# Full-array score matmuls over zero-padded operands, new orders, and one subtraction moved from VectorE to GpSimd

## The chip, the cores and the metric

One core of a Trainium2 chip runs the whole program. The metric is the device time of one execution in microseconds, the median of the runs shown.

## The reference

A pre-norm transformer layer on x of 16 sequences by 256 tokens by 256 features, in float32:

```python
x = x + attention(layernorm(x))      # 16 heads of 16; key j is masked where j - i > 16
x = x + ffn(layernorm(x))
# attention: q, k, v = z @ w.T ; softmax(q k^T / 4 + mask) v, then @ wo.T
# ffn: silu(z @ gate_w.T) * (z @ up_w.T) @ down_w.T, inner width 1024
# gate_w, up_w, down_w: cubic splines through 2033 control points each
```

## The kernel before, in words

**Turns.** One turn is one sequence of 256 tokens, so there are 16 turns (t). A turn is cut into steps: `la`, `lb` (layer norm), `zt` (transpose), `qk` (two halves of 8 heads), `v`, `ld` (DMAs that lay out the queries and keys), `s1` (scores for the row maximum, eight steps of two heads), `mt` (the maxima turned), `sc` (transposed scores and exponential, eight steps), `av` (weighted sums, four steps of four heads), `ot` (division and turning), `on` (splitting in high and low parts), `wo`, `ma`, `mb`, `z2`, `mo` (moments for the spline weights), `ga`, `up`, `ic`, `dn`, `y` (the feed-forward part and the result). Some nine tenths of the columns of TensorE are float32r matmuls in three products (high by high, high by low, low by high), so every operand is held as a rounded high part (ScalarE copies it) and a low remainder (a subtraction).

**Order.** Tables `START`, `OWN` and `TURN` give each step a number; the steps of all turns are sorted by it (`all_steps`), and each engine issues its share of every step in that order. Nothing reorders an engine's queue: a step whose input is late holds all behind it on that engine. Several turns are in work at once. In the middle turns a `s1` step of one turn and a `sc` step of the turn before follow each other on TensorE; such a pair is called a couple below.

**Scores.** A float32 product of 16 features in three terms is one contraction over 64 rows: every fourth partition holds the high part, the low part, or the high part again. `ld` (L661 to L671) fills `QM` and `KS`, each [128, slot of the turn, pair, 256], with 6 DMAs per half and 12 per turn; the slot is t % 2, so two turns have their own space. Two heads of a pair lie in partitions 0 to 63 and 64 to 127. A `s1` step (L1026 to L1035) and a `sc` step (L1042 to L1050) are four matmuls, two for each head, that use half the rows of the array each; the two heads write different banks of PSUM. `mt` (L1036, L904 to L909, L672 to L677) turns 16 columns twice, copies 16 by 256, and two DMAs put the negated maxima in row 63 of each half of `QM`, which `sc` multiplies with a row of ones in `KS`. PSUM gives these steps two places (`pairs`), each seeded with the mask by ScalarE before a `s1` step.

**Around them.** SP issues all DMAs: 12 for `ld`, 2 for `mt`, the loads `x` and `xr` and the store `y`: 17 in a turn, and 24 more (`pm`, L656) at the start. `on` is a copy on ScalarE and a subtraction on VectorE (L847). GpSimd does `affine_select` on the exponentials in two instructions after every second `sc` step (L732, L735), a power in `la` and `ma`, and the low half of `ic` (L740).

Of the kernel before, what the change touches and what calls it, by code (L numbers as in the profile page):

```python
# [7 lines left out]
F32 = mybir.dt.float32  # L8
# [7 lines left out]
H, DH = 16, 16  # L16
# [19 lines left out]
HP = NP // 2  # L36
DMA = 16
# [4 lines left out]
NQ = NW // 128  # L42
POWERS = 4
# [141 lines left out]
PERIOD = 29.3  # L185


def steps(table):

    return [(what, n + by * i, at + gap * i) for what, n, count, by, at, gap in table for i in range(count)]  # L190


START = [("fill", 0, 1, 1, -150.464, 0), ("hot", 0, 1, 1, -108.040, 0), ("in", 0, 1, 1, -104.078, 0),
             ("fill", 1, 1, 1, -103.866, 0), ("hot", 1, 1, 1, -101.965, 0), ("tap", 0, 1, 1, -86.665, 0),
             ("split", 0, 1, 1, -83.421, 0), ("in", 4, 1, 1, -81.659, 0), ("hot", 2, 1, 1, -72.688, 0),
# [3 lines left out]
             ("fill", 3, 1, 1, -49.605, 0), ("hot", 3, 1, 1, -45.788, 0), ("fill", 4, 1, 1, -45.146, 0),  # L199
# [3 lines left out]
             ("wj", 4, 1, 1, -33.201, 0), ("hot", 4, 1, 1, -29.039, 0), ("hot", 5, 1, 1, -26.819, 0),  # L203
# [939 lines left out]
```

## Time and profile before

| | |
|---|---|
| median of 3 runs | 530.36 us (530.16 to 531.9) |
| span of the profiled execution, first to last instruction | 529.3 us |
| its own device time beside the span | not given apart; the median is 1.1 us above the span |
| busy: PE, PEld, DVE, ACT, POOL | 507.1, 435.1, 425.4, 364.7, 211.9 us |
| mean granted TensorE clock | 0.987 |
| DMA: bytes, mean rate | 44.51 MB, 84 GB/s |

Busy is the union of an engine's instructions. Matmuls overlap in the pipeline, so their cost is read from start to start, not from their durations. Two matmuls that start within some nanoseconds of each other run side by side. SPq is SP's issuing of DMAs, which counts as no engine's busy time.

### The profile page before, as it was taken

The numbers are of one execution on the slowest core, as the hardware profiler recorded it, in microseconds if no ns is written. First come the engines' busy times: TensorE is split into PE (matmuls) and PEld (weight loads), VectorE is DVE, ScalarE is ACT, GpSimd is POOL, SyncE is SP. The second block draws the span as 40 slices with busy tenths as digits, with TensorE's granted clock in tenths as the row PEclk, the third lists the DMA queues.
The fourth block names the chain that finished last, engine by engine and source line by source line (L and its number), as shares of the span: only waits on it lengthen the run. The fifth ranks groups of instructions, "written<-read, shape, count | busy, mean of one in ns | idle before, by whom it ended". The sixth has DMA issues, their size and how long they took to land.

```text
span 529.3 us, 12741 instructions
## 1 busy us (share of the span) xinstructions
PE 507.1 (96%) x4840; PEld 435.1 (82%) x4840; DVE 425.4 (80%) x944; ACT 364.7 (69%) x536; POOL 211.9 (40%) x255
## 2 busy tenths in 40 slices
PE   7997979999999999999999999999999999999896
PEld 4665757898888898888888898988898888888785
DVE  4585679898898988898998998888988877777853
ACT  3366788676767778686877778686868777775522
POOL 4853345424343342424333352424343333435413
PEclk9898999999999999999999999999999999999999
DMA  8552332214032313131222123133212121300100
GB/s 257 202 179 69 125 101 73 70 50 145 28 113 73 99 62 122 63 120 63 89 84 75 58 81 102 62 100 102 82 60 81 46 78 37 106 2 22 41 21 20
DMA packets 45500, 44.51 MB, mean 84 GB/s; under 512 B 4736, under 2 KB 44544, under 8 KB 45440
## 3 DMA queue, kind: packets, MB, share of 16 engines
q1 hardware_dynamic: 45440, 43.70, 25.0%
q8 instruction: 39, 0.64, 0.5%
q14 instruction: 21, 0.17, 0.1%
HBM read 13.01 MB, written 4.19 MB: 33 GB/s over the span
## 4 chain that ended last, share of the span: by engine, by line
PE 70%; DVE 9%; SPq 9%; DMA 4%; issue 3%; ACT 3%; POOL 1%; POOLq 0%; DVEq 0%; ACTq 0%
PE ring L978 9%; PE ring L979 7%; PE ring L980 7%; PE ring L1056 7%; PE pair L1033 6%; PE pair L1048 6%; PE ring L1087 5%; SPq L670 4%; PE ring L1088 4%; PE ring L1089 4%; SPq L656 3%; DVE M L902 3%; PE ring L971 3%; PE ring L962 2%; PE ring L1076 2%
## 5 line engine op out<-in xcount | busy, mean ns | idle before, releaser
L806 ACT ACTIVATE P<-pair 128x800 f32<-128x800 f32 x128 | 106.4, 837 | 46.6 <-PE pair L1048 37.3
L902 DVE TENSOR_REDUCE M<-pair 128x2 f32<-128x288 f32 (+1 forms) x256 | 133.3, 565 | 2.9 <-PE pair L1033 2.7
L740 POOL TENSOR_TENSOR IN<-GU,IN 128x512 fp32r<-128x512 f32 x64 | 82.6, 1293 | 129.9 <-ACT IN L745 129.4
L745 ACT ACTIVATE pair<-SEED 128x800 f32<-128x800 bf16 x128 | 107.6, 842 | 14.1 <-DVE M L902 10.3
L732 POOL TENSOR_SCALAR_AFFINE_SELECT P<-P 128x448 f32<-128x448 f32 x64 | 37.3, 583 | 120.8 <-ACT P L806 120.8
L978 PE MATMUL ring<-WD,IN 128*128 128x256 f32 x256 | 76.4, 299 | 1.4 <-POOL IN L740 1.1
L1087 PE MATMUL ring<-Y,WGUh 128*128 128x256 f32 x256 | 76.2, 298 | 0.7 <-DVE Y L847 0.4
L1088 PE MATMUL ring<-Y,WGUh 128*128 128x256 f32 x256 | 72.0, 281 | 0.0
L1089 PE MATMUL ring<-Y,WGUl 128*128 128x256 f32 x256 | 71.8, 281 | 0.0
L979 PE MATMUL ring<-WD,IN 128*128 128x256 f32 x256 | 71.6, 280 | 0.0
L980 PE MATMUL ring<-WD,IN 128*128 128x256 f32 x256 | 71.6, 280 | 0.0
L745 ACT ACTIVATE IN<-GU 128x512 fp32r<-128x512 f32 x64 | 39.9, 627 | 29.5 <-DVE GU L948 28.9
L1048 PE MATMUL pair<-QM,KS 64*128 64x256 f32 (+1 forms) x512 | 53.5, 293 | 5.9 <-DMA QM<-MT 5.1
L1033 PE MATMUL pair<-KS,QM 63*128 63x256 f32 (+1 forms) x512 | 54.1, 294 | 3.0 <-ACT pair L745 1.5
L1087 PEld LDWEIGHTS ring<-Y,WGUh 128*128 128x128 f32 x256 | 48.2, 188 | 6.1 <-issue 3.0
L978 PEld LDWEIGHTS ring<-WD,IN 128*128 128x128 f32 x256 | 48.1, 188 | 5.7 <-issue 2.4
L1056 PE MATMUL ring<-P,V 128*32 128x256 f32 (+1 forms) x1024 | 52.2, 337 | 0.0
L1048 PEld LDWEIGHTS pair<-QM,KS 64*128 64x128 f32 x512 | 38.4, 188 | 16.6 <-issue 8.8
L1033 PEld LDWEIGHTS pair<-KS,QM 63*128 63x128 f32 x512 | 38.0, 186 | 15.9 <-ACT pair L745 6.2
L943 DVE SCALAR_TENSOR_TENSOR GU<-GU,ring 128x512 f32<-128x512 f32 x64 | 43.5, 681 | 8.7 <-ACT GU L831 7.7
L1089 PEld LDWEIGHTS ring<-Y,WGUl 128*128 128x128 f32 x256 | 48.2, 188 | 0.0
L1088 PEld LDWEIGHTS ring<-Y,WGUh 128*128 128x128 f32 x256 | 48.2, 188 | 0.0
(94 smaller groups left out, 1171.0 us busy)
## 6 DMA issues: line engine op xcount, KB each, us to landing
QM<-QK SPq DMA_DIRECT2D x96, 128.0 KB, 2.1
KS<-QK SPq DMA_DIRECT2D x96, 128.0 KB, 2.1
X<-x SPq DMA_DIRECT2D x32, 256.0 KB, 2.9
out<-X SPq DMA_DIRECT2D x16, 256.0 KB, 2.2
OVERD<-over_down SPq DMA_DIRECT2D x2, 512.0 KB, 7.6
PO<-W SPq DMA_DIRECT2D x16, 48.0 KB, 2.2
P<-wqk SPq DMA_DIRECT2D x2, 256.0 KB, 5.9
QM<-MT SPq DMA_DIRECT2D x32, 8.0 KB
```

Of the source, the lines that this page charges most:

```text
L745: copy = lambda dst, src: nc.scalar.activation(dst, src, ACT.Copy)
L806: nc.scalar.activation(P[:, g % 2, 2 * (n % 2):2 * (n % 2) + 2, :], pair(what, t, n)[:, :, 0:SW], ACT.Exp, scale=SCALE).then_inc(exp_done, 1)
L902: i = nc.vector.tensor_reduce(out=M[:, t % 2, it, :].rearrange("p (a k) -> p a k", a=2)[:, :, n], in_=pr[:, :, cols], axis=AX.X, op=ALU.ma ...
L978: mm(b, act(k, 0), w[:, k, 0:D], start=first and k == 0, stop=False, skip_group_check=True)
L979: mm(b, act(k, 0), w[:, k, D:2 * D], start=False, stop=False, skip_group_check=True)
L980: i = mm(b, act(k, 1), w[:, k, 0:D], start=False, stop=False, skip_group_check=True)
L1033: i = mm(pr[:, a, c:c + w], QM[r, t % 2, n, it * 128:(it + 1) * 128], KS[r, t % 2, n, 0:w], start=False, stop=it == 0, skip_group_check=True)
L1048: i = mm(pr[:, a, c:c + w], KS[r, t % 2, n, jt * 128:(jt + 1) * 128], QM[r, t % 2, n, S - w:S], start=jt == 0, stop=jt == 1, skip_group_ch ...
L1056: i = mm(bk[32 * hl:32 * hl + 32, S - w:S], V[:, t % 2, jt, n * 4 + hl, :, :].rearrange("p a c -> p (a c)"), P[:, n % 2, hl, c:c + w], sta ...
L1087: mm(o, wh, y[:, 0, g, :], start=j == 0, stop=False, skip_group_check=True)
L1088: mm(o, wh, y[:, 1, g, :], start=False, stop=False, skip_group_check=True)
L1089: i = mm(o, wl, y[:, 0, g, :], start=False, stop=False, skip_group_check=True)
```

## The change

- `s1` and `sc` are two matmuls each. The moving operand is a new tile, `KZ` and `QZ`, [128, 2, 4, 2, 256]: for head a of a pair only the 64 partitions of that head are filled, and the others hold zeros. One matmul with all 128 rows gives both heads side by side, 512 columns in one bank, and 288 in the next.
- Each of `QM`, `KS`, `QZ`, `KZ` has one copy in place of a slot per turn parity. `QK`, the source, has two. `ld` is 9 DMAs per half (three of 128 KB, six of 64 KB) and loads `QM` and `KZ`; it waits for `s1` of the turn before. A new step `lk` is 9 DMAs (three of 256 KB, six of 128 KB) for `KS` and `QZ`; it waits for all `sc` steps of the turn before. `mt` is one transpose of 128 columns, a copy of 32 by 128, and two DMAs into `QZ`.
- The subtraction of `on` goes from VectorE to GpSimd. `affine_select` is issued after every `sc` step over half the elements.
- `Z`, `OT` and `Y` have one copy instead of two. The small tiles of the layer norm have four.
- `START`, `OWN` and `TURN` have new numbers throughout.

```diff
-PERIOD = 29.3
+PERIOD = 29.4252
-TURN = [("x", 0, 1, 1, -56.556, 0), ("la", 0, 1, 1, -41.879, 0), ("lb", 0, 1, 1, -38.839, 0),
+TURN = [("x", 0, -90.4333), ("la", 0, -72.8908), ("lb", 0, -52.8920), ("zt", 0, -46.4935), ("qk", 0, -23.4598),
...
-        QM = sb("QM", [128, 2, NP, S], F32R)
-        KS = sb("KS", [128, 2, NP, S], F32R)
-        QK = sb("QK", [128, 2, 2, 2 * S], F32R)
+        QM, KS = (sb(n, [128, HP, 2, S], F32R) for n in ("QM", "KS"))
+        QZ, KZ = (sb(n, [128, 2, HP, 2, S], F32R) for n in ("QZ", "KZ"))
+        QK = [sb(f"QK{i}", [128, 2, 2, 2, S], F32R) for i in range(2)]
...
+        def heads_of(pr):
+            return ((pr[:, 0, :].rearrange("p (a c) -> p a c", a=2), S),
+                    (pr[:, 1, 0:2 * W1].rearrange("p (a c) -> p a c", a=2), W1))
...
                 elif what == "ld":
-                    sp.wait_ge(cleared, 4 if t else 2)
-                    if t >= 2:
-                        sp.wait_ge(sc_made, nth("sc", t - 2, n * HP + HP - 1))
+                    sp.wait_ge(cleared, 2)
+                    if t:
+                        sp.wait_ge(s1_made, nth("s1", t - 1, n * HP + HP - 1))
                     sp.wait_ge(qk_low, nth("qk", t, n))
...
+                    for k, part in enumerate(Q_PARTS):
+                        sp.dma_start(QM[k:128:4, :, n, :].bitcast(F32), QK[t % 2][:, part, 0, n, :].bitcast(F32)).then_inc(
+                            kz_loaded[n], DMA)
+                    for k, part in enumerate(K_PARTS):
+                        for a in range(2):
+                            r = slice(STACK * a, STACK * (a + 1))
+                            sp.dma_start(KZ[STACK * a + k:STACK * (a + 1):4, a, :, n, :].bitcast(F32),
+                                         QK[t % 2][r, part, 1, n, :].bitcast(F32)).then_inc(kz_loaded[n], DMA)
+                elif what == "lk":
+                    sp.wait_ge(cleared, 4)
+                    if t:
+                        sp.wait_ge(sc_made, nth("sc", t - 1, NP - 1))
+                    sp.wait_ge(qk_low, nth("qk", t, 1))
+                    for k, part in enumerate(K_PARTS):
+                        sp.dma_start(KS[k:128:4].rearrange("p j h c -> p j (h c)").bitcast(F32),
+                                     QK[t % 2][:, part, 1].rearrange("p h c -> p (h c)").bitcast(F32)).then_inc(ks_loaded, DMA)
+                    for k, part in enumerate(Q_PARTS):
+                        for a in range(2):
...
                 elif what == "mt":
                     sp.wait_ge(mt_done, nth("mt", t, 0))
+                    if t:
+                        sp.wait_ge(sc_made, nth("sc", t - 1, NP - 1))
...
-                elif what == "sc" and n % 2:
+                elif what == "sc":
...
+                elif what == "on":
+                    pool.wait_ge(on_high, nth("on", t, 0))
+                    low(OTT[:, 1, :, :], OT[:, 0:KB, :], OTT[:, 0, :, :]).then_inc(on_low, 1)
...
                 elif what == "s1":
-                    for it, c, w in ((1, W0, S), (0, 0, W0)):
-                        for a in range(2):
-                            r = slice(STACK * a, STACK * a + STACK - 1)
-                            i = mm(pr[:, a, c:c + w], QM[r, t % 2, n, it * 128:(it + 1) * 128], KS[r, t % 2, n, 0:w],
-                                   start=False, stop=it == 0, skip_group_check=True)
+                    h, j = divmod(n, HP)
+                    if j == 0:
+                        pe.wait_ge(kz_loaded[h], N_LOAD * (t + 1))
+                    for it, (o, w) in zip((1, 0), heads_of(pair(what, t, n))):
+                        i = mm(o, QM[:, j, h, it * 128:(it + 1) * 128], KZ[:, :, j, h, 0:w], start=False, stop=True, skip_group_check=True)
...
                 elif what == "sc":
+                    h, j = divmod(n, HP)
                     if n == 0:
-                        pe.wait_ge(m_loaded[t % 2], N_M * (t // 2 + 1))
+                        pe.wait_ge(ks_loaded, N_LOAD * (t + 1))
+                        pe.wait_ge(m_loaded, N_M * (t + 1))
+                    for jt, (o, w) in enumerate(heads_of(pair(what, t, n))):
+                        i = mm(o, KS[:, j, h, jt * 128:(jt + 1) * 128], QZ[:, :, j, h, S - w:S], start=True, stop=True)
```

How the order moves is shown at two places of a middle turn. First TensorE, where the turned maxima of the turn stand. `KS,QM` is a `s1` step and `QM,KS` a `sc` step of the kernel before; `P,V` is `av`, `ID,M` the transposes of the maxima, `WD,IN` a `dn` step. `Y,WGUh` and `Y,WGUl` belong to `ga` and `up`. Before, a couple stands between an `up` and a `dn` step:

```order
L1089 MATMUL ring<-Y,WGUl 128x256
L1033 MATMUL pair<-KS,QM 128x256 x2
L1033 MATMUL pair<-KS,QM 128x144 x2
L1048 MATMUL pair<-QM,KS 128x256 x2
L1048 MATMUL pair<-QM,KS 128x144 x2
L978 MATMUL ring<-WD,IN 128x256
```

Of the change (`KZ,QM` is `s1`), the maxima stand next to `av`:

```order
L1050 MATMUL ring<-Y,WGUl 128x256
L998 MATMUL pair<-KZ,QM 128x512
L998 MATMUL pair<-KZ,QM 128x288
L1002 MATMUL ring<-ID,M 128x128
L1017 MATMUL ring<-P,V 32x256 x4
L1017 MATMUL ring<-P,V 32x144 x4
L1017 MATMUL ring<-P,V 32x256 x4
L1017 MATMUL ring<-P,V 32x144 x4
L998 MATMUL pair<-KZ,QM 128x512
L998 MATMUL pair<-KZ,QM 128x288
L945 MATMUL ring<-WV,ZT 128x256
```

A score step went from four rows to two, and the couples are mostly dissolved: of 256 steps, 132 runs of neighbouring score steps became 227. `av` has 42 runs before and 43 now; 24 of them directly followed a score step before, with no change of the array's shape in between.

Second SP, one middle turn. Before:

```order
L684 DMA out<-X 128x2x256
L681 DMA X<-x 128x2x256
L670 DMA QM<-QK 32x4x256 x3
L670 DMA KS<-QK 32x4x256 x3
L660 DMA X<-x 128x2x256
L676 DMA QM<-MT 1x8x256 x2
L670 DMA QM<-QK 32x4x256 x3
L670 DMA KS<-QK 32x4x256 x3
```

Of the change:

```order
L639 DMA X<-x 128x2x256
L619 DMA KS<-QK 32x4x512 x3
L624 DMA QZ<-QK 16x4x512 x6
L599 DMA X<-x 128x2x256
L642 DMA out<-X 128x2x256
L634 DMA QZ<-MT 1x16x128 x2
L606 DMA QM<-QK 32x4x256 x3
L611 DMA KZ<-QK 16x4x256 x6
L606 DMA QM<-QK 32x4x256 x3
L611 DMA KZ<-QK 16x4x256 x6
```

SP issues 32 DMAs in a turn instead of 17, and between the last `sc` step of one turn and the first of the next now stand nine of `lk`, one or two of x and out, and the two of the maxima.

## Rows read from the trace of the kernel before

**Rows 1.** The page, part 1: busy time, share of the span, instructions.
```profile
...
PE 507.1 (96%) x4840; PEld 435.1 (82%) x4840; DVE 425.4 (80%) x944; ACT 364.7 (69%) x536; POOL 211.9 (40%) x255
```

**Rows 2.** Windows: busy PE, PEld, DVE, ACT, POOL (instructions), clock, DMA share, GB/s.
```profile
...
0.00:20.00 20.00, 17.25 (x79) 11.29 (x80) 10.70 (x26) 6.08 (x9) 11.65 (x14) 0.83 0.79 264
236.00:265.00 29.00, 29.00 (x292) 25.51 (x291) 25.52 (x59) 21.66 (x33) 11.18 (x14) 1.00 0.23 74
500.00:529.00 29.00, 22.27 (x176) 20.85 (x174) 13.82 (x26) 8.53 (x15) 8.71 (x8) 1.00 0.06 19
```

**Rows 3.** Timeline of PE around one couple of score steps: start, duration, instruction, count.
```profile
...
246.32 0.28 PE L1088 MATMUL ring<-Y,WGUh 128*128 128x256 f32 x1
246.44 0.28 PE L1089 MATMUL ring<-Y,WGUl 128*128 128x256 f32 x1
246.65 0.45 PE L1033 MATMUL pair<-KS,QM 63*128 63x256 f32 x4
246.94 0.39 PE L1048 MATMUL pair<-QM,KS 64*128 64x256 f32 x4
247.26 0.39 PE L978 MATMUL ring<-WD,IN 128*128 128x256 f32 x1
247.48 0.28 PE L979 MATMUL ring<-WD,IN 128*128 128x256 f32 x1
```

**Rows 4.** Timeline of PE, a run of full-array bf16 matmuls of 256 columns.
```profile
...
19.96 1.49 PE L992 MATMUL ring<-HEAT 128*128 128x256 bf16 x12
```

**Rows 5.** Timeline of PE: a double weighted sum, the maxima's transposes; the next turn's.
```profile
...
240.76 0.28 PE L1089 MATMUL ring<-Y,WGUl 128*128 128x256 f32 x1
240.97 1.56 PE L1056 MATMUL ring<-P,V 128*32 128x256 f32 x32
242.46 0.39 PE L1039 MATMUL ring<-ID,M 128*16 128x128 f32 x2
242.83 0.39 PE L1087 MATMUL ring<-Y,WGUh 128*128 128x256 f32 x1
243.06 0.28 PE L1088 MATMUL ring<-Y,WGUh 128*128 128x256 f32 x1
...
271.95 0.39 PE L1039 MATMUL ring<-ID,M 128*16 128x128 f32 x2
```

**Rows 6.** Groups by line and shape: busy us, mean ns of one, idle before.
```profile
...
L847 DVE TENSOR_TENSOR OTT<-OT,OTT 128x512 fp32r<-128x512 f32 x16 | 11.8, 737 | 1.8 <-ACT OTT L745 1.3
...
L909 DVE CAST MT<-ring 16x256 fp32r<-16x256 f32 x16 | 6.1, 383 | 1.1 <-PE ring L1039 1.1
...
L745 ACT ACTIVATE OTT<-OT 128x512 fp32r<-128x512 f32 x16 | 10.1, 631 | 6.5 <-DVE OT L925 6.5
...
L740 POOL TENSOR_TENSOR IN<-GU,IN 128x512 fp32r<-128x512 f32 x64 | 82.6, 1293 | 129.9 <-ACT IN L745 129.4
```

**Rows 7.** Timeline of SP, the DMA issues of one stretch.
```profile
...
258.74 0.39 SPq L684 DMA_DIRECT2D out<-X  x1
...
263.62 2.70 SPq L670 DMA_DIRECT2D KS<-QK  x3
266.37 0.59 SPq L660 DMA_DIRECT2D X<-x  x1
273.29 1.43 SPq L676 DMA_DIRECT2D QM<-MT  x2
274.83 1.88 SPq L670 DMA_DIRECT2D QM<-QK  x3
```

**Rows 8.** The chain that ended last, at the maxima's load in turn 2.
```profile
...
97.23 1.95 DMA QM<-MT
...
99.32 0.69 PE pair L1048 x8
```

**Rows 9.** Windows: the stretch with most DMA traffic beside the loads.
```profile
...
289.20:293.00 3.80, 3.80 (x34) 3.55 (x35) 3.30 (x7) 3.71 (x6) 0.79 (x2) 1.00 0.83 273
```

**Rows 10.** Waits of PE from 120 to 440 us: total, times, longest.
```profile
...
PE pair L1048 <- DMA QM<-MT: 0.2, 1, 0.2
```

More of the change, by code:

```diff
@@ L36 @@
 HP = NP // 2
+EDGE = 2 * S
+PS = 2 * SW
 DMA = 16
@@ L398, in all_steps @@
 def all_steps():
-    out = [(at, what, 0, n) for what, n, at in steps_of_start()]
-    out += [(t * PERIOD + at, what, t, n) for t in range(TURNS) for what, n, at in steps_of_turn(t)]
+    out = [(at, what, 0, n) for at, what, n in steps_of_start()]
+    out += [(t * PERIOD + at, what, t, n) for t in range(TURNS) for at, what, n in steps_of_turn(t)]
     return [i[1:] for i in sorted(out, key=lambda i: i[0])]
@@ L530, in build @@
         GU = sb("GU", [128, 2, 2 * S])
-        Y = [sb(f"Y{i}", [128, 2, 3, S], F32R) for i in range(2)]
+        Y = sb("Y", [128, 2, 3, S], F32R)
+        YT = sb("YT", [128, 2, KB, S], F32R)
         ring = [ctx.enter_context(nc.psum_tensor(f"ring{i}", [128, 512], F32)) for i in range(4)]
@@ L542, in build @@
         mo_made, mo_high, mo_low = map(sem, ("mo_made", "mo_high", "mo_low"))
-        qk_loaded = [[sem(f"qk_loaded{s}{h}") for h in range(2)] for s in range(2)]
-        m_loaded = [sem(f"m_loaded{s}") for s in range(2)]
+        kz_loaded = [sem(f"kz_loaded{h}") for h in range(2)]
+        ks_loaded, m_loaded = map(sem, ("ks_loaded", "m_loaded"))
         xr_loaded, y_stored = ([sem(f"{n}{i}") for i in range(N_X1)] for n in ("xr_loaded", "y_stored"))
@@ L781, in _ @@
                     act.wait_ge(qk_made, nth("qk", t, n))
-                    if t:
-                        act.wait_ge(qk_loaded[(t - 1) % 2][n], N_QK * ((t - 1) // 2 + 1))
-                    copy(QK[:, n, 0, :], bank(what, t, n)[:]).then_inc(qk_high, 1)
+                    if t >= 2:
+                        act.wait_ge(kz_loaded[n], N_LOAD * (t - 1))
+                        act.wait_ge(ks_loaded, N_LOAD * (t - 1))
+                    copy(QK[t % 2][:, 0, :, n, :], halves(bank(what, t, n)[:])).then_inc(qk_high, 1)
                 elif what == "v":
@@ L797, in _ @@
                         act.wait_ge(*emptied(BEFORE["s1", t, n]))
[L798 removed]
+                    copy(scores(pair("s1", t, n)), SEED[:]).then_inc(seeded, 1)
                 elif what == "sc":
@@ L811, in _ @@
                         act.wait_ge(wo_made, nth("wo", t - 1, 0))
-                    copy(OTT[:, 0, :, :], OT[t % 2][:, 0:KB, :]).then_inc(on_high, 1)
+                    copy(OTT[:, 0, :, :], OT[:, 0:KB, :]).then_inc(on_high, 1)
                 elif what == "z2":
                     act.wait_ge(z2_made, nth("z2", t, 0))
+                    if t == 0:
+                        act.wait_ge(permuted, 24 * DMA)
                     if t:
@@ L822, in _ @@
                         act.wait_ge(ws_low, GATE_UP)
-                    if t >= 2 and n == 0:
-                        act.wait_ge(up_made, nth("up", t - 2, 3))
+                    if t and n == 0:
+                        act.wait_ge(up_made, nth("up", t - 1, 3))
                     g = slice(2, 3) if n else slice(0, 2)
-                    copy(Y[t % 2][:, 0, g, :], moments(bank(what, t, n), n)).then_inc(mo_high, 1)
+                    copy(Y[:, 0, g, :], moments(bank(what, t, n), n)).then_inc(mo_high, 1)
                 elif what == "ga":
@@ L894, in _ @@
                     dve.wait_ge(qk_high, nth("qk", t, n))
-                    low(QK[:, n, 1, :], bank(what, t, n)[:], QK[:, n, 0, :]).then_inc(qk_low, 1)
+                    low(QK[t % 2][:, 1, :, n, :], halves(bank(what, t, n)[:]), QK[t % 2][:, 0, :, n, :]).then_inc(qk_low, 1)
                 elif what == "s1":
                     dve.wait_ge(s1_made, nth("s1", t, n))
-                    pr = pair("s1", t, n)
+                    if n == 0 and t == 0:
+                        dve.wait_ge(m_cleared, 1)
                     if n == 0 and t >= 2:
                         dve.wait_ge(mt_made, nth("mt", t - 2, 0))
-                    for it, cols in ((0, slice(0, W0)), (1, slice(W0, W0 + S))):
-                        i = nc.vector.tensor_reduce(out=M[:, t % 2, it, :].rearrange("p (a k) -> p a k", a=2)[:, :, n],
-                                                    in_=pr[:, :, cols], axis=AX.X, op=ALU.max, negate=True)
+                    for it, (o, w) in zip((1, 0), heads_of(pair("s1", t, n))):
+                        k = n % HP * 4 + n // HP * 2 + it
+                        i = nc.vector.tensor_reduce(out=M[:, t % 2, 0:2 * H].rearrange("p (a k) -> p a k", a=2)[:, :, k],
+                                                    in_=o, axis=AX.X, op=ALU.max, negate=True)
                     i.then_inc(max_done, 1)
@@ L1132 @@
         "ident": np.eye(128, dtype=np.float32),
-        "seed": np.concatenate([np.zeros((128, AHEAD)), upper, np.zeros((128, W0)), upper[:, :J1]], axis=1).astype(ml_dtypes.bfloat16),
+        "seed": np.concatenate([np.zeros((128, W0)), upper[:, :J1]] * 2 + [np.zeros((128, AHEAD)), upper] * 2, axis=1).astype(ml_dtypes.bfloat16),
     }
```

143 lines of the change are left out of this document (66 added, 77 removed), and 297 rows, old and new, of tables (OWN, START, TURN).

## The prediction

> **What bounds the kernel now.** I read the page's busy times first: TensorE 96%, VectorE 80%, ScalarE 69%, GpSimd 40% [rows 1]. The windows say where. In a middle turn TensorE is busy all of the 29 us, at a granted clock of 1.00, and VectorE 25.5 of it; in the first 20 us it has 17.25 us at clock 0.83, and in the last 29 us 22.27 [rows 2]. From 120 to 440 us the only wait that TensorE has on a DMA is 0.2 us, for the maxima [rows 10]. So in the middle the work that TensorE has per turn is the time per turn: the transposes of the maxima of neighbouring turns start at 242.46 and 271.95, 29.49 us apart [rows 5]. What shortens TensorE's queue shortens the kernel, unless something else becomes late; what changes on VectorE or GpSimd alone does not.
>
> **The score steps.** Full-array matmuls of 256 columns start 0.12 us apart (246.32, 246.44). After the last, the couple should start at 246.56. It starts at 246.65, its second step at 246.94, the next full matmul at 247.26, and the one behind that only at 247.48 instead of 0.12 later [rows 3]. The couple thus holds the engine from 246.56 to 247.48 - 0.12 = 247.36: 0.80 us. The step itself is some 0.23 us, and 0.35 us of the 0.80 is the passage into half-array work (0.09) and out of it (0.26, of which 0.10 shows only on the second full matmul). 128 couples make 102.4 us. 24 runs go straight on to a weighted sum, which is also narrow, and save the 0.10 once: 100 us.
>
> After, a step is 512 and 288 columns on the whole array, without a passage. At the pace of the full float32r matmuls (0.12 for 256) that is 0.37 us; at 2.4 GHz and one column a cycle 800 columns need 0.33 us. The bf16 matmuls of 256 columns are nearer to the latter: 12 of them span 1.49 us, of which the last one's own pipeline is some 0.28, so they start 0.11 apart [rows 4]. The float32r ones lose 0.01 more on each, and a matmul twice as long pays that once for 512 columns. I take 0.35, so 256 steps make 89.6 us, with 84.5 to 94.7 as bounds. **Gain 10.4 us.**
>
> The rule that speaks against this stands in the Trainium skill, "TensorEngine Tiling (Array Packing)", section "Theoretical Speedup": with a contraction of at most 64 rows, row tiling gives up to twice the speed, so giving it up should cost. The rows show why it need not: the two halves do run side by side (a step of 800 columns in all in 0.23 us), but the passages take back more than that. The same page, "Key Properties", says that changing the mode drains the engine; by that rule, the trace agrees, with the 0.35 us per couple.
>
> **Weighted sums and maxima.** `av` stays narrow. Two steps take from 240.97 to 242.46, and entering costs 0.21 - 0.12 = 0.09 [rows 5]. Before, 24 of its 42 runs came from a score step and paid no entry; now all 43 do: 25 x 0.09 = 2.2 us, and six more exits at 0.10: 0.6 us. **Loss 2.8 us.** Of the two transposes of the maxima one goes: 16 x 0.12 = 1.9 us, and where the narrow shape left late (242.46 to 242.83 for two, then 0.23) another 0.2 in some turns: **gain 2.4 us.** TensorE's queue is thus shorter by 10.4 - 2.8 + 2.4 = **10 us**, with bounds of 5 and 15 from the step's. In a middle turn this is 0.6 us.
>
> **VectorE, GpSimd, ScalarE.** VectorE loses 16 subtractions of 0.737 us and about 0.1 us per copy of the maxima [rows 6]: under the full TensorE this is worth nothing. GpSimd takes 1.293 us for such a subtraction of 128 by 512 [rows 6], so `wo` gets its input 0.56 us later. In a middle turn 6.8 us of other work stand on TensorE between the last weighted sum and `wo` (`v` and two `qk` of 12 matmuls each, four score steps, a `mo` and a `ga`), and the chain of transposes, division, copy and subtraction adds to 4 us, or 6.2 with two reductions between. Cover is left; without it 0.56 x 16 = 9 us would be lost. GpSimd has 11.2 of 29 us busy [rows 2] and goes to some 14: nothing. The single `Z`, `OT` and `Y` are asked for 7 us or more after they come free in the new table: nothing. ScalarE has the same 800 elements per seed and exponential.
>
> **SP and the single buffers.** This is the change's cost. An issue takes 0.62 us (three in 1.88), one of the maxima's 0.71, one of out 0.39, one of x 0.59 [rows 7]. 32 issues are 20 us of a turn of 29, so SP is not full. But `lk` may only start when the last `sc` step of the turn before has ended, and the maxima's DMAs are behind it. The chain from the end of the last `sc` to the first `sc` of the next turn: 0.35 to see the matmul's end; nine issues 5.6; x or out or both 0.4 to 1.0; the first maxima DMA's issue 0.74; the second's issue and landing 1.95, and 0.14 until TensorE starts [rows 8]. Together 9.2 to 9.8 us. In that time TensorE has, by the new order of the middle turns, two `up` steps, three `s1` steps, the maxima, two weighted sums, a fourth `s1`, `v`, two `qk`, a `mo` and a `ga`: 10 us. That covers it barely. It fails where the order has less: turn 2 (9.6 us of work, two loads of x), turn 13 (8.9), turn 15 (8.9), and turn 1, where six `pm` DMAs stand in between (13.2 against 11.5). I add 1.7 + 0.3 + 0.6 + 0.2 = 2.8 us. One issue in about 25 takes 0.4 to 1.7 us longer (2.70 for three at 263.62) [rows 7]; with 12 issues in each of 15 chains that is some 6 us, half of it covered: 2.7. **Loss 5.5 us**, lower bound 0 (all covered), upper bound in the rival below.
>
> **Start and end.** New orders there too. The fills before the first `ld` grow from two memsets to the size of three, while GpSimd waits for weights anyway. SP's queue until the maxima of turn 1 has some 80 issues instead of 64, but 12 of the 24 `pm` move behind them. By the same issue times the first `sc` of turn 2 comes at about 95 to 101 us, against 99.32 now [rows 8]. The last turn has 5 us more of TensorE work behind its maxima, but was a stretch with 7 us idle [rows 2]. I set both at 0, from -4 to +5.
>
> **Sum.** 529.3 - 10 + 5.5 = 524.8 us of span, and with the 1.1 us by which the median of the runs lies above the span, **525.9 us**, 0.8% under 530.36.
>
> **Rivals.**
> *The single buffers hold TensorE in every turn (slower).* For it: the loads of `lk` are 1.5 MB, with x and out 2 MB in 6.5 us, 310 GB/s, and the densest stretch now moved 273 GB/s at a DMA share of 0.83 [rows 9], so at most 329. If the queue runs at 273, the maxima land 1 us later or more; and if a `lk` issue costs 0.71 like those of the maxima, 0.8 us comes on top. 1.2 us over the cover in 15 turns is 18 us in place of 5.5: 538 us. It decides from 0.65 us per turn, where TensorE's 10 us are gone. Against: 64-partition transfers may be issued faster, and half the excess comes with HBM transfers that do not stand in every chain.
> *The packing was worth its passages.* If a full step costs twice the 0.23 us of the packed one, 256 x 0.46 = 118 us against 100: the queue grows by 18 instead of shrinking by 10, 554 us. Against: the columns of the full matmuls around it go at 0.12 for 256, which leaves no room for it. This is the tiling page's twofold speed taken at its word.
> *All of it comes through.* Steps at 0.33 us, waits covered, a start 3 us earlier: 529.3 - 15 + 1 - 3 + 1.1 = 513 us. For it: VectorE is relieved, and the order was laid out for these lengths.
> *No change beyond measurement.* Gains and waits cancel: 530.4 us. Likewise if the matmul's gain is at its lower bound of 5.
>
> **How the numbers follow.** A measurement of this kernel tells about 0.3% from no change: 528.8 to 532.0. Forecast 0.52, all through 0.13, no change 0.13, held by the single buffers 0.19, packing 0.03. Of the forecast's own spread (step 0.33 to 0.37, start and end) little lies above 528.8. So faster 0.65, same 0.13, slower 0.22. The range takes in the forecast's bounds and most of the first rival: 514 to 538 us.
>
> **What would show it.** Right: score steps of 0.34 to 0.36 us from start to start with full matmuls 0.12 us before and behind them; middle turns of 28.8 to 29.2 us; waits of TensorE on the load into `QZ`, some 5 us in all; the first `sc` of turn 2 near 98 us. The forecast is wrong if a wait on `QZ` stands in every middle turn, if middle turns stay at 29.5 with TensorE full (the step is dearer than 0.37), or if the first maxima of turn 2 are turned much after 95 us.

## The result, and the profile after

The changed kernel takes 538.78 us (median of 4 runs, 537.08 to 541.22), beside 530.38 for the kernel before on the same chip: a ratio of 1.015, 95% interval 1.0118 to 1.0183. It is 1.5% slower, where 525.9 was forecast, and lies 0.8 us above the range. The profiled execution took 537.08 us, its span is 535.4 against 529.3: 6.1 of the 8.4 us can be looked for in the traces. Of the other 2.3, 1.7 us are that the profiled execution was quicker than the median of its kernel. Of the kernels' executions shown here all are in the fast state; one more of `e5_packed`, of 1585 us, was in the slow one and is left out.

The busy line of the profile's page, to be read against [rows 1]:

```profile
...
PE 503.7 (94%) x4312; PEld 441.7 (83%) x4312; DVE 428.9 (80%) x929; ACT 356.2 (67%) x536; POOL 256.3 (48%) x399
```

TensorE has 3.4 us less of busy time in a span that is 6.1 us longer. So the idle time grew, and the windows tell where (columns as in [rows 2]):

```profile
...
0.00:20.00 20.00, 8.29 (x38) 5.50 (x38) 11.66 (x19) 4.00 (x5) 8.44 (x10) 0.78 0.53 179
236.00:265.00 29.00, 28.74 (x263) 26.34 (x262) 25.12 (x58) 21.20 (x33) 13.55 (x24) 1.00 0.43 143
...
0.00:192.36 192.36, 168.77 (x1275) 134.92 (x1276) 147.70 (x318) 122.76 (x183) 96.57 (x140) 0.95 0.46 150
```

In the first 20 us TensorE has 8.29 us of work done, before it was 17.25. The middle turn is nearly full, as before. The last row reaches to the maxima of turn 5: TensorE has 23.6 us without work in it. In the kernel before it has 12.2 up to the same place.

A place in the program that both kernels have is the transpose of the maxima (L1039 before, L1002 after). Its times cut the span into three:

| us | turn 5's maxima | turn 15's maxima | end | 0 to turn 5 | ten turns | rest |
|---|---|---|---|---|---|---|
| before | 184.1 | 473.7 | 529.3 | 184.1 | 289.6 | 55.6 |
| after | 192.4 | 480.2 | 535.4 | 192.4 | 287.8 | 55.2 |
| difference | | | | **+8.3** | **-1.8** | -0.4 |

**The loss is made before turn 5**, where the forecast has a zero. The first `sc` of turn 2 comes at 107.5 us, not at 95 to 101.

The marks cut the span by time and not by work, and the order is new. Counted in the traces, the changed kernel has less ahead of turn 5's maxima: two steps of `av`, 12 matmuls of `dn`, 12 of `ga` and `up`, 4 of `mo` and 24 of `qk`, against one `s1` step more. At the paces of a middle turn that is some 7 us of work (an estimate). It has some 2 us more between the two marks and 5 us more behind them. So 8.3 us is the least that the start lost, and the ten turns gained more than 1.8.

Four turns hold the same matmuls in both kernels but for the score steps and the maxima: from turn 6's maxima to turn 10's. The windows for the kernel before, for the changed one, and for the run `e6_issue_order` below, where TensorE never waits in them:

```profile
...
213.00:331.00 118.00, 118.00 (x1181) 104.09 (x1178) 105.08 (x239) 89.06 (x129) 45.48 (x58) 1.00 0.25 82
```

```profile
...
222.90:339.30 116.40, 114.99 (x1046) 105.74 (x1044) 101.44 (x231) 84.84 (x128) 54.34 (x92) 1.00 0.41 135
```

```profile
...
219.10:333.80 114.70, 114.70 (x1047) 105.63 (x1045) 101.52 (x231) 84.68 (x128) 54.37 (x92) 1.00 0.41 137
```

Without a wait a turn is 0.83 us shorter than before. With the waits of the changed kernel 0.4 us of it are left.

**The start, first part.** TensorE's waits in the whole run (total, times, longest):

```profile
...
PE ring L929 <- DVE X L856: 10.5, 1, 10.5
PE pair L1009 <- DMA QZ<-MT: 6.1, 8, 1.4
```

One wait of 10.5 us, on the normalised `X` (before 0.9). VectorE and GpSimd in that time (start, duration, instruction, count):

```profile
...
6.18 0.75 DVE L843 BATCH_NORM_STATS2 ST<-X 128x6 f32<-128x256 f32 x2 [4.71 <-DMA X<-x]
...
9.38 7.16 DVE L856 TENSOR_SCALAR X<-X,MV,RSTD 128x256 f32<-128x256 f32 x4 [0.81 <-POOL RSTD L659]
```

```profile
...
9.64 1.26 POOL L649 TENSOR_TENSOR WQKl<-P,WQKh 128x512 fp32r<-128x512 f32 x1 [0.30 <-ACT WQKh L708]
10.85 3.65 POOL L662 MEMSET KZ<- 128x4096 f32 x1
14.45 1.95 POOL L662 MEMSET QM<- 128x2048 f32 x1
```

```profile
...
L856 DVE TENSOR_SCALAR X<-X,MV,RSTD x4: 411/1660/3674, 9.4 to 14.6; 128x256 f32<-128x256 f32 x4
```

Four normalisations of 128 by 256 take 7.16 us. The shortest is 0.411 us, the other three are 1.352, 3.674 and 1.967 us, and beside them lie GpSimd's subtraction (1.26 us) and its two memsets (3.65 and 1.95 us). The pairs match in length and in time. The Trainium skill, "SBUF — State Buffer", section "Who interferes with whom", has the rule: a `tensor_scalar` on VectorE can run in a mode that uses the port pair shared with GpSimd, and whichever of the two is issued first holds it for the whole instruction. The trace agrees: the memset of 3.65 us begins at 10.85, the normalisation behind it at 10.98, and that ends 0.15 us after the memset. In the kernel before, both memsets (1.80 us each) were over by 4.50 us, ahead of VectorE's first normalisation at 6.07. In the new table they stand behind GpSimd's share of the layer norm. Also, `X` of turn 0 is now the third transfer and turn 1 is normalised first, so VectorE starts at 6.18 instead of 3.48 us.

TensorE had nothing to do from 6.2 to 16.7 us. Its granted clock fell to 1.2 GHz at 11.2 us and was back at 2.4 GHz at 25 us, so its first work ran at the lower one, with full matmuls of 256 columns 0.21 us apart and not 0.12. In the kernel before it was also down, from 11.0 to 17.8 us, and both kernels have short stretches of it later. Up to turn 5 TensorE was busy for 15.0 us at the lower clock, before for 13.7. Nearly half of such time is lost, so the clock itself explains some 0.7 us of the difference (an estimate).

**The start, second part.** SP's queue (issues: start, duration, count), and its waits from 20 to 105 us, after and then before:

```profile
...
65.53 3.14 SPq L611 DMA_DIRECT2D KZ<-QK  x5
68.78 2.14 SPq L619 DMA_DIRECT2D KS<-QK  x3
70.96 4.19 SPq L624 DMA_DIRECT2D QZ<-QK  x6
75.19 4.05 SPq L595 DMA_DIRECT2D PO<-W  x6
79.29 0.58 SPq L599 DMA_DIRECT2D X<-x  x1
79.97 1.18 SPq L634 DMA_DIRECT2D QZ<-MT  x2
81.19 7.58 SPq L595 DMA_DIRECT2D PO<-W  x12
```

```profile
...
SPq L599 <- PE ring L929: 3.7, 1, 3.7
SPq L617 <- PE pair L1009: 1.5, 1, 1.5
SPq L634 <- DVE MT L879: 0.6, 2, 0.3
```

```profile
...
SPq L665 <- PE pair L1048: 15.0, 3, 8.5
SPq L660 <- PE ring L962: 11.0, 1, 11.0
SPq L676 <- DVE MT L909: 2.9, 2, 2.7
SPq L665 <- DVE QK L847: 1.8, 2, 1.6
```

Before, SP waited for others for 30.7 of these 85 us, with 83 issues that took 52.3 us. After, it has 118 issues of 73.3 us in all and waits 5.8 us: from 25 us on it is nearly always behind. The 12 moves into `WP` (`PO<-W` in the rows) at 81.19, and six more at 75.19, stand between the loads for the scores.

**The middle.** A score step between full matmuls (as [rows 3]), and the chain from the loads of `KS` to the first `sc` of turn 7 (start, duration, piece):

```profile
...
235.52 0.28 PE L1050 MATMUL ring<-Y,WGUl 128*128 128x256 f32 x1
235.64 0.53 PE L1009 MATMUL pair<-QZ,KS 128*128 128x512 f32 x2
236.01 0.28 PE L1048 MATMUL ring<-Y,WGUh 128*128 128x256 f32 x1
236.13 0.28 PE L1049 MATMUL ring<-Y,WGUh 128*128 128x256 f32 x1
```

```profile
...
250.01 0.55 SPq L619
...
251.91 0.60 SPq L624
...
257.25 0.56 SPq L634
...
257.86 2.33 DMA QZ<-MT
...
260.32 0.47 PE pair L1009
```

The step holds the engine from 235.64 to 236.01, 0.37 us, and the matmul behind it starts 0.12 later as it should: there is no passage any more. In the chain, `KS` is issued from 250.01, 0.35 us after the `sc` that it waits for, and TensorE starts at 260.32: 10.7 us, the last 0.3 of them a wait; the longest such wait in the run is 1.4 us.

### The profile page after: what moved, and what is told of

It is laid out like the page before. It is cut to its first block, busy times and chain, and to the rows that moved or that the text cites. A ratio compares the mean times of both kernels' runs of the same rounds, so it can differ in the third digit from the quotient of the medians.

```text
span 535.4 us, 12091 instructions
## 1 busy us (share of the span) xinstructions
PE 503.7 (94%) x4312; PEld 441.7 (83%) x4312; DVE 428.9 (80%) x929; ACT 356.2 (67%) x536; POOL 256.3 (48%) x399
## 4 chain that ended last, share of the span: by engine, by line
PE 67%; SPq 16%; DVE 6%; DMA 5%; issue 3%; ACT 2%; POOL 1%; DVEq 0%
PE pair L1009 8%; PE ring L945 7%; PE ring L946 7%; PE ring L947 7%; PE pair L998 6%; PE ring L1017 6%; SPq L624 5%; PE ring L1048 5%; PE ring L1050 5%; PE ring L1049 5%; DMA QZ<-MT 4%; SPq L611 3%; SPq L619 3%; PE ring L929 2%; PE ring L1037 2%
## 5 line engine op out<-in xcount | busy, mean ns | idle before, releaser
L872 DVE TENSOR_REDUCE M<-pair 128x2 f32<-128x512 f32 (+1 forms) x256 | 132.4, 564 | 9.8 <-PE pair L998 8.7
L692 POOL TENSOR_SCALAR_AFFINE_SELECT P<-P 128x224 f32<-128x224 f32 x128 | 49.2, 385 | 125.9 <-ACT P L770 125.8
L703 POOL TENSOR_TENSOR IN<-GU,IN 128x512 fp32r<-128x512 f32 x64 | 81.9, 1294 | 55.4 <-ACT IN L708 55.2
L998 PE MATMUL pair<-KZ,QM 128*128 128x512 f32 (+1 forms) x256 | 72.6, 368 | 5.8 <-ACT pair L708 3.7
L1009 PE MATMUL pair<-QZ,KS 128*128 128x512 f32 (+1 forms) x256 | 70.5, 361 | 7.0 <-DMA QZ<-MT 6.1
L1048 PE MATMUL ring<-Y,WGUh 128*128 128x256 f32 x256 | 72.4, 283 | 0.0
L945 PE MATMUL ring<-WD,IN 128*128 128x256 f32 x256 | 72.1, 281 | 0.1
L946 PE MATMUL ring<-WD,IN 128*128 128x256 f32 x256 | 72.0, 281 | 0.0
L947 PE MATMUL ring<-WD,IN 128*128 128x256 f32 x256 | 71.8, 280 | 0.0
L1049 PE MATMUL ring<-Y,WGUh 128*128 128x256 f32 x256 | 71.6, 280 | 0.0
L998 PEld LDWEIGHTS pair<-KZ,QM 128*128 128x128 f32 x256 | 39.1, 189 | 18.8 <-ACT pair L708 10.0
L695 POOL TENSOR_SCALAR_AFFINE_SELECT P<-P 128x256 f32<-128x256 f32 x128 | 53.8, 420 | 0.0
L1009 PEld LDWEIGHTS pair<-QZ,KS 128*128 128x128 f32 x256 | 39.6, 191 | 13.3 <-issue 7.9
L945 PEld LDWEIGHTS ring<-WD,IN 128*128 128x128 f32 x256 | 48.1, 188 | 1.8 <-issue 0.2
L947 PEld LDWEIGHTS ring<-WD,IN 128*128 128x128 f32 x256 | 48.2, 188 | 0.0
```

The lines of the kernel that those rows point to most:

```text
L872: i = nc.vector.tensor_reduce(out=M[:, t % 2, 0:2 * H].rearrange("p (a k) -> p a k", a=2)[:, :, k], in_=o, axis=AX.X, op=ALU.max, negate=True)
L945: mm(b, act(k, 0), w[:, k, 0:D], start=first and k == 0, stop=False, skip_group_check=True)
L946: mm(b, act(k, 0), w[:, k, D:2 * D], start=False, stop=False, skip_group_check=True)
L947: i = mm(b, act(k, 1), w[:, k, 0:D], start=False, stop=False, skip_group_check=True)
L998: i = mm(o, QM[:, j, h, it * 128:(it + 1) * 128], KZ[:, :, j, h, 0:w], start=False, stop=True, skip_group_check=True)
L1009: i = mm(o, KS[:, j, h, jt * 128:(jt + 1) * 128], QZ[:, :, j, h, S - w:S], start=True, stop=True)
```

## The experiments

The theories after the result. *Start*: the port pair and the order of the first transfers, then SP's full queue. *Rival 1*: the single buffers hold TensorE all along. *Rival 2*: the packing was worth more than its passages. *Rival 3*: GpSimd's subtraction is not free. All ratios are to the kernel before on the same chip, with 95% intervals; its median there was 530.4 to 531.9 us. Beside the times, the table gives the turns' marks as above, all runs but `e4` in the changed kernel's order on TensorE. The marks are those of one profiled execution each, and executions of one kernel differ (those of e2 by 7 us), so what a run is worth is read from its ratio, and a mark says where it was gained.

| run | time, us | ratio | turn 5 | turn 15 | span |
|---|---|---|---|---|---|
| after | 538.78 | 1.015 [1.0118, 1.0183] | 192.4 | 480.2 | 535.4 |
| e1_fills_first | 534.29 | 1.0025 [0.9998, 1.0052] | 189.4 | 479.1 | 534.3 |
| e2_start_order | 532.08 | 0.9994 [0.9965, 1.0023] | 188.1 | 474.6 | 530.0 |
| e3_on_vector | 537.56 | 1.0098 [1.0062, 1.0134] | 190.9 | 478.9 | 534.3 |
| e4_order_before | 601.55 | 1.1278 | 231.4 | 540.0 | 601.2 |
| e5_packed | 562.23 | 1.0558 [1.0511, 1.0606] | 195.6 | 502.0 | 557.0 |
| e6_issue_order | 531.03 | 0.9988 [0.9967, 1.001] | 189.1 | 473.1 | 528.6 |
| e7_ks_scalar | 536.06 | 1.0095 [1.0065, 1.0125] | 193.4 | 480.6 | 536.0 |
| e8_pm_scalar | 541.91 | 1.0189 [1.0155, 1.0223] | 199.5 | 486.4 | 542.0 |
| e9_pm_once | 527.98 | 0.993 [0.9903, 0.9957] | 185.1 | 469.0 | 524.2 |
| e10_merged_loads | 524.97 | 0.9872 [0.9843, 0.99] | 185.7 | 469.4 | 524.3 |
| e11_best | 530.6 | 0.9978 [0.9957, 0.9999] | 187.3 | 471.3 | 526.6 |

### The memsets first

```diff
-START = [... ("fill", 0, -141.4603), ... ("fill", 1, -135.8028),
+START = [... ("fill", 0, -500.0), ... ("fill", 1, -499.0),
```

> The changed kernel with its first two fills (KZ, QM) put at the head of GpSimd's queue, ahead of the powers of the first two layer norms. Theory A (the start: the fills run beside VectorE's first normalisations, and each of these lasts as long as the fill beside it, 1.4, 3.7 and 2.0 us instead of 0.41): the four normalisations take 1.6 us instead of 7.2, the first transposes start at about 11 us instead of 16.7, and the time falls by 4 to 6 us, to 533 to 535 us. Theory B (the start is bound by SP's queue of loads, or the middle by the single buffers): the transposes are earlier but the first sc step stays where it is, and the time falls by 1 us at most.

```profile
...
0.96 3.51 POOL L662 MEMSET KZ<- 128x4096 f32 x1
4.40 1.80 POOL L662 MEMSET QM<- 128x2048 f32 x1
...
9.23 1.27 POOL L649 TENSOR_TENSOR WQKl<-P,WQKh 128x512 fp32r<-128x512 f32 x1 [0.33 <-ACT WQKh L708]
```

```profile
...
8.94 2.36 DVE L856 TENSOR_SCALAR X<-X,MV,RSTD 128x256 f32<-128x256 f32 x4 [0.81 <-POOL RSTD L659]
```

With the memsets over at 6.2 us, the four normalisations take 2.36 us instead of 7.16, and what is left of the excess stands beside GpSimd's subtraction at 9.23. The maxima of turn 5 come 3.0 us earlier. The interval of the ratio lies wholly under that of the changed kernel, and the ratios are 1.25% apart, 6.6 us. This part of the cause is shown.

### The first transfers and turns in order

```diff
-("in", 9, -128.5907), ("in", 0, -118.0497), ...
+("in", 0, -460.0), ("in", 4, -459.0), ("in", 9, -458.0), ("in", 1, -457.0), ...
-1: [("la", 0, -414.6793), ("lb", 0, -247.8181),
+1: [("la", 0, -121.4), ("lb", 0, -119.4),
```

> As the run before it, and the loads at the start in the order of the kernel before (x, TAP, powers, seed, ident, wqk ...) and turn 1's first layer norm behind turn 0's transposes. Theory A (the start): first transposes at 7 to 8 us, 3 us more than the run before gained, so 529 to 532 us. Theory B: no more than 1 us against the changed kernel.

TensorE's first transposes now start at 7.9 us (16.7 in the changed kernel, 6.95 before), and turn 5 comes another 1.3 us earlier. In the first 100 us this did not carry through in full: SP still had hardly a pause from 21 to 96 us. In the marks of turn 5 the two runs together give back 4.3 us. By the ratios it is more: 1.0150 has become 0.9994, 8.3 us, with both intervals clear of the changed kernel's. That is as much as the changed kernel was slower. Against e1 alone, e2's intervals overlap, so the share of the transfers' order is not told from nothing by the times; the earlier first transposes show it.

### The subtraction back on VectorE

```diff
 elif what == "on":
-    pool.wait_ge(on_high, nth("on", t, 0))
+    dve.wait_ge(on_high, nth("on", t, 0))
     low(OTT[:, 1, :, :], OT[:, 0:KB, :], OTT[:, 0, :, :]).then_inc(on_low, 1)
```

> The changed kernel with the subtraction of on back on VectorE, order numbers untouched. If the move to GpSimd costs anything (wo waits for GpSimd, or the division's product on VectorE lasts as long as the GpSimd work beside it, 1.0 to 1.5 us instead of 0.43 in 7 places), the time falls by 1 to 3 us. My prediction's reading (nothing on either side, TensorE full): within 1 us of the changed kernel, 538 to 540 us.

The span is 1.1 us shorter and the ratio 0.5% lower, and the intervals of the two ratios overlap: this run does not tell the move's cost from nothing. The one wait on `OTT` from 120 to 440 us (0.6 us) is gone.

### The order of before

```diff
-PERIOD = 29.4252
+PERIOD = 29.3
-START = [...]   -OWN = {...}   -TURN = [...]
+START, OWN and TURN with the numbers of the kernel before, and lk just ahead of mt
```

> The changed kernel (full-array matmuls, single buffers, on on GpSimd) with the order numbers of the kernel before; lk stands just ahead of mt, and the first half of qk is put 3 to 7 us later from turn 3 on, because it now waits for lk. If the new orders are what costs: the start is as early as before (first transposes at 7 us), the middle turns are 29.1 to 29.5 us, and the time is 530 to 534 us. If the single buffers are what costs: in the old order TensorE has only 8.9 us of work between the last sc of a turn and the first of the next, against a chain of 9.3 to 9.8, so each turn waits 0.5 us or more and the time is 536 to 542 us, no better than the changed kernel.

With the single buffers under the old order the kernel takes some 70 us more than before, far more than either theory had. TensorE waits 35.1 us on `QZ` in 8 turns, up to 12.5 in one, and another 11.8 us on VectorE's maxima. The first four turns take 36 to 41 us from maxima to maxima, most of the middle ones 30.1 to 30.4. So the new order is no addition to the change: without it the single buffers are dear. The run mixes several causes, since `qk` also had to be moved, and gives no price for one of them.

### The packed score steps in the new order

```diff
-for it, (o, w) in zip((1, 0), heads_of(pair(what, t, n))):
-    mm(o, QM[:, j, h, it * 128:(it + 1) * 128], KZ[:, :, j, h, 0:w], ...)
+for it, c, w in ((1, W0, S), (0, 0, W0)):
+    for a in range(2):
+        r = slice(STACK * a, STACK * (a + 1))
+        mm(pr[:, a, c:c + w], QM[r, j, h, it * 128:(it + 1) * 128], KZ[r, a, j, h, 0:w], ...)
```

> The changed kernel in all (new orders, single buffers, loads, GpSimd's subtraction, one transpose of the maxima), with the score steps alone packed as before: two half-array matmuls side by side per column block. Theory (the passages cost what full-array steps save): in the new order the score steps stand mostly by themselves between other work, so a packed step pays its own entry and exit of 0.35 us: 0.23 + 0.35 = 0.58 against the 0.367 us measured for a full step, 0.21 us on most of 256 steps less what is saved where a narrow weighted sum follows: some 20 to 30 us more on TensorE, 557 to 568 us. Rival (the packing was worth its passages, and the change lost it): the packed kernel is faster than the changed one, below 536 us. Rival (no difference worth naming, the loss is wholly in order and start): 536 to 542 us.

```profile
...
238.91 0.28 PE L947 MATMUL ring<-WO,OTT 128*128 128x256 f32 x1
239.12 0.45 PE L1016 MATMUL pair<-QZ,KS 64*128 64x256 f32 x4
239.50 0.39 PE L1056 MATMUL ring<-Y,WGUh 128*128 128x256 f32 x1
239.73 0.28 PE L1057 MATMUL ring<-Y,WGUh 128*128 128x256 f32 x1
```

Full matmuls start 0.12 us apart. Without the step the next would start at 239.03; with it the pace is back at 239.73 - 0.12 = 239.61. A packed step by itself holds the engine 0.58 us, as expected, the full one 0.37. The kernel is 21.6 us slower by the spans (557.0 to 535.4), so rival 2 falls, and the matmul part of the change is worth more in this order than in the old one, where a couple of steps shared its passages. A packed step has 0.23 us between its borders, the full one 0.37, and the borders take 0.35. The twofold speed of the Trainium skill, "TensorEngine Tiling (Array Packing)", section "Theoretical Speedup", is thus there in part inside the step, and for 800 columns it does not pay its borders.

### SP's issues in another order

The loads of x, the stores and the moves of `WP` that stood between the loads of `lk` and those of the maxima go behind them (with the start of e2).

```diff
-for what, t, n in STEPS:
+for what, t, n in sp_steps():   # between lk and mt: x, xr, y, pm go behind mt
```

> As the run with the start's transfers in order, and on SP's queue the loads of x, the stores of y and the moves of WP that stood between the loads of KS and the maxima's are issued behind the maxima's. Theory (in the middle the chain from the last sc step over SP's issues to the first sc step of the next turn holds TensorE by some 4 us in all): the waits on the load of QZ shrink from 3.7 us to under 2, and the time falls by 1 to 3 us, to a ratio near 0.995. Rival (the middle is bound by TensorE alone, the chain is covered): within 1 us of that run, ratio 0.998 to 1.001.

```profile
...
PE pair L1025 <- DMA QZ<-MT: 1.4, 2, 0.9
```

The wait on `QZ` falls from 3.7 us to 1.4, and from turn 5 to 15 there is none. Five middle turns are 28.62 to 28.75 us long, which is TensorE's work of a turn without a pause; before, [rows 5] show 29.49. The ten turns take 284.0 us, 2.5 less than in e2 and 5.6 less than before. The span is 1.4 us shorter, since 1.0 was lost at the start. That the order removes these waits is shown; that the kernel gains by it is not. The ratio went from 0.9994 to 0.9988, where 0.995 was expected, and that is the rival's reading.

### Issues moved from SP to ScalarE

```diff
 # e7, on ScalarE behind the exponential of sc 7 of the turn before
+for k, part in enumerate(K_PARTS):
+    nc.scalar.dma_start(KS[k:128:4]..., QK[(t + 1) % 2][:, part, 1]...)
 # e8, on ScalarE at pm's place, for steps 2 and 3
+nc.scalar.dma_start(WP[8 * a:8 * a + 16, j0:j0 + nt, :], W[...])
```

> As the run with the start's transfers in order, and the three loads of KS are issued by ScalarE's queue behind the exponential of the last sc step of the turn before, from turn 1 on; SP keeps three issues less per turn. Theory (SP's queue is full from 21 to 96 us and stands in the chain after): the first sc of turn 3 comes 3 to 6 us earlier than at 136.2, the waits on QZ fall below 2 us, time 2 to 6 us shorter, ratio 0.989 to 0.996. Rival (SP's queue does not bound the start, VectorE and TensorE work do): first sc of turn 3 within 1.5 us of 136.2, ratio 0.998 to 1.001. Rival (the issues cost ScalarE more than SP gains): exponentials of the last steps late, slower, ratio over 1.003.

> As the run with the start's transfers in order, and the moves into WP of steps 2 and 3 (12 of the 24 transfers) are issued from ScalarE's queue. Theory (SP's queue bounds 60 to 105 us): twelve issues of 0.6 us leave SP, the stall of TensorE between 80 and 100 us shrinks from 8.6 us to under 5, first sc of turn 3 at 131 to 134 instead of 136.2, ratio 0.991 to 0.996. Rival (the start is bound by other work): first sc of turn 3 within 1 us, ratio 0.998 to 1.001.

```profile
...
70.00 4.55 ACTq L728 DMA_DIRECT2D PO<-W  x5
74.67 0.60 ACT L708 ACTIVATE ZT<-ring 128x512 fp32r<-128x512 f32 x1 [4.13 <-issue]
...
84.26 3.78 ACTq L728 DMA_DIRECT2D PO<-W  x6
88.15 1.57 ACT L782 ACTIVATE P<-pair 128x800 f32<-128x800 f32 x2 [5.34 <-issue]
```

Both are slower, by 1.0% and 2.0% against e2. In e8 each group of six issues stops ScalarE for some 4 us (a hole of 4.13 us ahead of `ZT`, and one of 5.34 ahead of the exponentials, of which the issues fill 3.78), and SP then waited 18 us for a score step that those held up. In e7 ScalarE's seeds came late in the first turns (waits of TensorE on them 6.1 us, in e2 3.0). SP was relieved and the place was the wrong one, so these two do not speak to SP's own part. A run was needed that takes issues away and gives them to nobody.

### Fewer issues

```diff
 # e9: one move of the same bytes per step of pm, in place of six
+sp.dma_start(WP[8 * a:8 * a + 32, :, :], W[:, (n + GATE_UP) % 4, 0:2 * D])
 # e10: both heads in one transfer, no zero half (KZ; QZ alike)
+sp.dma_start(KZ[k:128:4, 0, :, n, :]..., QK[t % 2][:, part, 1, n, :]...)
```

> As the run with the order of issues on SP, but each step of the moves from W into WP is one transfer instead of six (the same bytes, laid down straight: the permutation of the down weights is left out, so this part of the result is another). 20 issues of 0.6 us, 12 us, leave SP between 50 and 95 us. Theory (SP's full queue at the start holds the first turns, and what happened with the issues given to ScalarE was ScalarE's own delay): the first maxima of turn 3 are turned 3 to 8 us earlier than at 132.7 us, of turn 5 at 182 to 186 instead of 189.1, ratio 0.985 to 0.994. Rival (the loss at the start is work and order on TensorE, VectorE and ScalarE): turn 5 within 1.5 us of 189.1, ratio 0.997 to 1.001.

> As the run with the order of issues on SP, but the loads of KZ and QZ go for both heads in one transfer into plane 0 (the same bytes and matmuls; the zero padding is left out, so scores are sums over two heads): 3 issues less for each ld and for lk, 9 of 32 per turn, 144 in all. Theory (the issues that padding adds bound the start, and a little of the middle): turn 5's maxima at 181 to 185 us instead of 189.1, middle turns 28.6 us with no wait on QZ, ratio 0.982 to 0.991. Rival (the issues are covered but for the chain of lk): turn 5 within 1.5 us, 1 us less in the middle, ratio 0.996 to 0.999.

```profile
...
SPq L646 <- DVE MT L891: 5.9, 4, 2.0
SPq L608 <- POOL W L695: 5.6, 1, 5.6
SPq L616 <- PE pair L1010: 4.6, 2, 4.4
```

```profile
...
SPq L646 <- DVE MT L891: 20.9, 4, 6.1
SPq L620 <- PE pair L1010: 8.9, 2, 6.0
SPq L620 <- DVE QK L824: 4.0, 3, 2.9
SPq L631 <- PE pair L1021: 2.5, 2, 2.3
```

e9 leaves out the permutation of the down weights and e10 the zero halves, so both serve for the time alone. They bring turn 5 to 185.1 and 185.7 us (189.1 in e6), though the one removes issues of the weights and the other issues of the padding. By the ratios they are 0.6% and 1.2% faster than e6, with intervals clear of its own. What they have in common is SP: it waits for others for 22 and 36 us (the rows above and three smaller ones of e9) of the stretch from 20 to 140 us, in e6 for 12. So SP's queue was a bound of the start. The bytes and the matmuls are the same, so it was the number of transfers, at some 0.6 us each, and not what they carry.

The granted clock has a part in e9. Up to turn 5 TensorE was busy at 1.2 GHz for 20.1 us in e6, for 12.9 in e9 and for 18.5 in e10. Half of the difference is 3.6 us for e9, most of what its mark shows, and 0.8 for e10. Whether the clock stayed up because SP's queue was shorter is not shown, so e10 is the cleaner evidence. In e10 no wait on a DMA is left from turn 5 to 15.

### The best of them

The issue order of e6, and the subtraction on VectorE.

```diff
-for what, t, n in STEPS:
+for what, t, n in sp_steps():
-    pool.wait_ge(on_high, nth("on", t, 0))
+    dve.wait_ge(on_high, nth("on", t, 0))
```

> As the run with the order of issues on SP, and the subtraction for the turned heads back on VectorE. From the run that undid this alone (1 us faster than the changed kernel): 529.5 to 530.5 us, ratio 0.995 to 0.998. Rival (VectorE, now 25 us busy of a turn of 28.6, becomes late itself): ratio 1.000 to 1.004, with turns above 28.7 us.

The span is 526.6 us, 2.0 under e6, and the ratio 0.9978 with an interval that just ends below 1. It is 0.2% under the kernel before at best, and the measurement hardly tells that from no change. Against the changed kernel it is 1.7% faster by the ratios.

## Why the prediction was wrong

**The step that failed** is "Start and end": "I set both at 0, from -4 to +5". By the mark of turn 5 the start cost 8.3 us. By the sum it is more: the span is 10.6 us above the forecast's 524.8, and the waits on `QZ` are 0.6 us of this, so some 10 us are the start's if TensorE's queue got shorter as forecast (an estimate).
- "The fills before the first `ld` grow from two memsets to the size of three, while GpSimd waits for weights anyway." I looked at who waits for GpSimd, and not at who runs beside it, nor at their new place in the order. They went behind the arrival of `X` and held VectorE's normalisation, TensorE's first input. With the order of the first transfers this was 8.3 us by the ratios, 4.3 by the marks (e1, e2).
- "SP's queue until the maxima of turn 1 has some 80 issues instead of 64." I counted the issues and took the first `sc` of turn 2 from them alone, at 95 to 101 us. It came at 107.5. The wait row of SP would have told that it had 30.7 us to spare before in 85; 35 more issues of 0.6 us and the late begin used it up. Fewer issues gave a further 3 us (e9) and 6 us (e10) by the ratios against e6, and 3 to 4 by the marks, with the clock's part in e9.
- With both out of the way the forecast's time is there: e10 has a ratio of 0.987 and a span of 524.3 us. It leaves out the padding's transfers, so it is not the change as it was forecast.
- For the end the 0 held: 55.6 and 55.2 us from turn 15's maxima on. TensorE's idle time there went from 8.0 to 4.1 us, which is how 5 us more work found room.

**The score step.** "I take 0.35": it is 0.37, at my upper bound, so 256 steps are some 94 us and not 89.6. The gain on TensorE's queue was still not smaller than forecast. I read one couple, at 0.80 us. From start to start the eight couples of the turn from 242.5 us hold the engine 6.4 us, two of them 0.84 and 0.85, where 100 us in sixteen turns makes 6.25. The one transpose fewer saves 0.26 us in such a turn, not 0.15. In the four turns above, 0.83 us per turn is gained, where 0.6 was forecast. Over the ten turns TensorE is busy 287.6 us before and 283.1 in e6, with some 2 us more work in them: 0.65 us per turn. For sixteen turns that makes 10 to 13 us (an estimate), beside the forecast's 10. That the error of the step was made good by others is luck. That the passages go and that the full matmuls around keep their 0.12 held. That a packed step by itself pays 0.35 us at its borders held too.

**Weighted sums, VectorE, GpSimd, single `Z`, `OT`, `Y`.** The entry into a weighted sum is again nearly 0.09: it starts at 240.81 behind a step at 240.36 (0.45 - 0.37). The moves on VectorE and GpSimd were set at nothing; e3 gives 1 us by the spans and e11 2 us, and neither is told from nothing by the intervals. Among the waits from 120 to 440 us none is on `Z`.

**The single buffers.** The chain is 10.7 us long, not 9.2 to 9.8: the landing of the last transfer took 2.33 us, where [rows 8] have 1.95, and one issue was 0.3 us late. TensorE's waits on `QZ` sum to 6.1 us in 8 turns; 5.5 were forecast. Of this, 3.1 us lie between turn 5 and 15, and with 0.8 on GpSimd the waits there are 3.9 us, where the kernel before has 1.8. The term of 5.5 us for the single buffers thus held.

**The 1.1 us.** I added the 1.1 us by which the median lies above the profiled span. In the executions of all other runs the time is 1.7 to 1.9 us above the span, so the profiled execution of the kernel before was probably a slower one than its median. This moves the forecast by 0.7 us at most.

**The rivals.** The first (held in every turn, 538 us) has the measured time but not the mechanism: its sign was a wait on `QZ` in every middle turn, and half of the turns have none. The time alone would have confirmed it. The packing rival (554 us) was wrong in sign. That all comes through (513 us) failed at the start, which was to be 3 us earlier.

## What to carry to other kernels

A change that pays per turn in the steady state has a start of its own: forecast it by its own queue, first input first, and before more issues are put on a queue read how long that queue waits for others, since that is all it can take. Where two engines share a port, the place of an otherwise free instruction decides: put memsets before the data lands. Issuing from a compute engine is no relief where that engine's results are on the path; fewer and larger transfers are.

## What was not expected of the hardware

- VectorE's 128 by 256 normalisation of 0.41 us takes 3.67 us beside a memset of 3.65 us on GpSimd, although the two share no data.
- The same holds for a product of two operands in SBUF:

```profile
...
165.87 1.31 DVE L892 TENSOR_TENSOR Z<-OT,R 128x256 f32<-128x256 f32 x1
```

```profile
...
165.62 1.29 POOL L703 TENSOR_TENSOR IN<-GU,IN 128x512 fp32r<-128x512 f32 x1 [3.03 <-ACT IN L708]
```

It takes 0.43 us elsewhere in the run and 1.31 here, and it ends 0.27 us after the GpSimd product of 1.29 us. Seven of its 32 instances took over 1.0 us, each beside such a product; in the kernel before it was one. The same section of the Trainium skill, "SBUF — State Buffer", says that a VectorE instruction with two inputs in SBUF contends with a GpSimd instruction that reads SBUF; the trace agrees. The seven lost some 6 us of VectorE's time; whether the kernel lost any was not tried.
- Six transfers issued from ScalarE hold its own work for about 4 us: in e8 its next activation comes when the last of the six issues is through, at 74.67 and at 88.15 us.
